# SyncE issues the second minus-maximum's rows ahead of two weight blocks, and the K parts lie in DRAM by dimension, batch and head

## What is computed

```
x = x + tanh(g_xattn[0]) * fp8_blockwise_product(layernorm(x), ctx)      # L0 "attention"
x = x + tanh(g_ffn[0])   * moe_8_experts_top2_plus_shared(layernorm(x))  # L0 feed-forward
x = x + tanh(g_xattn[1]) * causal_attention(layernorm(x), ctx, ctx)      # L1, 16 heads of 16
x = x + tanh(g_ffn[1])   * moe_8_experts_top2_hidden_1024(layernorm(x))  # L1 feed-forward
```

```
scores = einsum('bhqd,bhkd->bhqk', qh, kh) / 4
scores = where(causal, scores, -10000)
out    = einsum('bhqk,bhkd->bhqd', softmax(scores), vh)
```

## Time and profile before

| | us |
|---|---|
| median of 3 runs | 411.5 |
| lowest, highest | 411.11, 413.36 |
| the profiled execution | 412.41 |
| its span, first to last instruction | 410.6 |
| outside the span | 1.8 |
| DMA queue q1 (SyncE's), share of 16 engines | 40.2% |

### The profile page before, as it was taken

The page is one execution under the profiler, slowest core; times in us unless marked ns, Lnnn a source line. Parts: engine busy times, 40 slices in busy tenths (PEclk is TensorE's granted clock), DMA queues, the critical chain, the costliest instruction groups (busy, mean ns, idle before and its releaser), DMA issues.

```text
span 410.6 us, 8728 instructions
## 1 busy us (share of the span) xinstructions
PE 321.0 (78%) x2708; PEld 222.1 (54%) x2709; DVE 306.0 (75%) x745; ACT 268.2 (65%) x540; POOL 180.4 (44%) x245
## 2 busy tenths in 40 slices
PE   0075989989799986878777224698999999999991
PEld 0053337664377654556444113475777777777760
DVE  4998997783954663897998885586777777888760
ACT  1825766725676486989798665652677777777770
POOL 3051305391384067433747459410444554444432
PEclk9997999989989998999977756697999999999997
DMA  5950002851095069130416449455677777778522
GB/s 176 388 222 0 2 0 107 126 147 59 4 225 158 15 85 221 46 117 2 119 42 206 126 102 329 154 219 177 184 254 248 255 200 255 210 253 254 154 26 26
DMA packets 27298, 60.48 MB, mean 147 GB/s; under 512 B 4305, under 2 KB 17954, under 8 KB 24066
## 3 DMA queue, kind: packets, MB, share of 16 engines
q1 hardware_dynamic: 20658, 53.20, 40.2%
q0 software_dynamic: 4416, 6.13, 9.3%
q10 hardware_dynamic: 2192, 0.75, 0.7%
HBM read 29.00 MB, written 6.85 MB: 87 GB/s over the span
## 4 chain that ended last, share of the span: by engine, by line
PE 42%; DVE 28%; DMA 10%; issue 9%; ACT 8%; POOL 2%; ACTq 1%; SPq 0%; DVEq 0%; POOLq 0%
PE bank L1270 8%; PE bank L1637 6%; PE bank L1655 6%; DMA out_dram<-arena,SI 5%; DVE MX L2000 3%; PE bank L1640 3%; PE bank L1658 3%; DMA STG<-in_l_w_dram 2%; PE bank L1356 2%; PE bank L1231 2%; DMA arena<-NMS 2%; PE bank L1382 2%; DVE stats L1720 2%; PE bank L1378 1%; ACT arena L1131 1%
## 5 line engine op out<-in xcount | busy, mean ns | idle before, releaser
L1655 PE MATMUL bank<-arena 128*128 x184 | 63.4, 390 | 2.6 <-DVE X L2274 1.1
L1131 ACT ACTIVATE arena<-arena,B1D 128x128 f32<-128x128 f32 x184 | 57.4, 391 | 8.6 <-DVE arena L2287 8.1
L2287 DVE TENSOR_REDUCE arena<-bank 128x256 f32<-128x512 f32 x92 | 57.3, 680 | 3.1 <-PE bank L1640 3.1
L685 POOL TENSOR_TENSOR W<-STG,W 128x256 f16<-128x256 f32 x64 | 42.7, 700 | 33.4 <-ACT W L882 28.9
L782 POOL DMA_INDIRECT out_dram<-arena,SI x23 | 36.4, 1584 | 36.2 <-DMA out_dram<-arena,SI 16.9
L1658 PE MATMUL bank<-arena 128*128 x184 | 51.3, 279 | 0.0
L685 POOL TENSOR_TENSOR arena<-STG,arena 128x256 f16<-128x256 f32 x56 | 37.3, 700 | 30.2 <-ACT arena L882 28.8
L1637 PE MATMUL bank<-arena 128*128 128x256 f16 x256 | 46.4, 282 | 1.6 <-DVE arena L2250 1.6
L769 POOL DMA_INDIRECT arena<-token_rows,GI x23 | 22.8, 993 | 53.3 <-ACT WS L1125 45.1
L2292 DVE SCALAR_TENSOR_TENSOR arena<-arena 128x512 f16<-128x512 f32 x46 | 29.7, 688 | 21.8 <-ACT arena L1138 21.8
L1640 PE MATMUL bank<-arena 128*128 128x128 f16 x256 | 45.3, 225 | 0.0
(11 more groups left out here) (280 smaller groups left out, 722.3 us busy)
## 6 DMA issues: line engine op xcount, KB each, us to landing
STG<-in_l_w_dram SPq DMA_DIRECT2D x32, 512.0 KB, 4.0
arena<-W SPq DMA_DIRECT2D x16, 1024.0 KB
STG<-W SPq DMA_DIRECT2D x7, 1024.0 KB
arena<-in_l_w_dram SPq DMA_DIRECT2D x2, 1280.0 KB, 7.5
k_parts<-W SPq DMA_DIRECT2D x2, 768.0 KB, 4.4
arena<-k_parts SPq DMA_DIRECT2D x12, 128.0 KB, 5.2
X<-in_x_dram SPq DMA_DIRECT2D x2, 512.0 KB, 7.4
W<-in_ctx_dram SPq DMA_DIRECT2D x1, 1024.0 KB, 10.2
```

Of the source, the lines that this page charges most:

```text
L685: ins = nc.gpsimd.tensor_tensor(l, src, h, ALU.subtract)
L1131: ins = nc.scalar.activation(x, x, ACT.Gelu, bias=B1D[:, e, c:c + 1], scale=1.0 / (X_SCALE * W_SCALE))
L1655: nc.tensor.matmul(bank[6 + q][:, :], GDL[:, q, 0, c * P:(c + 1) * P], W2[:, e, c].rearrange("p s d -> p (s d)"), start=(c == 0), stop=Fal ...
L2287: v.tensor_reduce(half, o, AX.X, ALU.add).then_inc(s_dadd, 1)
```

## The change

Two edits. In SyncE's stream load_minus_max(1) now stands right behind stack 2, ahead of weight blocks 14 and 15. And the DRAM tensor k_parts gets the shape [part, dimension, batch, head, token]: what one row of a stack needs is 8 KB in one run, where it was 16 runs of 512 bytes. The store writes six DMAs, one for each half and part, with 512-byte runs (it was two DMAs with 2 KB runs), and the waits on it count to 96 instead of 32.

```diff
-        k_parts = nc.dram_tensor("k_parts", [3, D, N], BF16).ap()
+        k_parts = nc.dram_tensor("k_parts", [3, DH, B, HEADS, S], BF16).ap()
...
             for k in range(KC):
-                sp.dma_start(k_parts[:, k * P:(k + 1) * P, :].rearrange("s p n -> p s n"),
-                             KS[:, :, k]).then_inc(s_kparts_out, 16)
-            sp.wait_ge(s_kparts_out, 16 * KC)
+                for s in range(3):
+                    sp.dma_start(k_parts[s, :, :, k * HH:(k + 1) * HH].rearrange("d b h n -> h d b n"),
+                                 KS[:, s, k]).then_inc(s_kparts_out, 16)
+            sp.wait_ge(s_kparts_out, 48 * KC)
...
-                    src = k_parts[s, :, b * S:(b + 1) * S].rearrange("(h d) n -> d h n", d=DH)
+                    src = k_parts[s, :, b]
...
             sp.wait_ge(s_down, T)
             load_k_stack(2)
+            load_minus_max(1)
             for i in range(14, 16):
                 load_weights(i)
-            load_minus_max(1)
             load_k_stack(3)
...
-            pool.wait_ge(s_kparts_out, 16 * KC)
+            pool.wait_ge(s_kparts_out, 48 * KC)
...
-                    act.wait_ge(s_kparts_out, 16 * KC)
+                    act.wait_ge(s_kparts_out, 48 * KC)
```

## The result

| | before | after |
|---|---|---|
| median of the runs taken together, us | 412.89 (20 runs) | 414.96 (20 runs) |
| profiled execution, us | 412.41 | 416.61 |
| its span, us | 410.6 | 414.8 |
| outside the span, us | 1.8 | 1.8 |

The ratio after / before is 1.0065, 95% interval 1.0039 to 1.009. A median is of all executions of a kernel, a ratio of those alone in which the chip was not in its slower state, so the two need not agree exactly. The change costs 0.65%, some 2.7 us, where the forecast was +0.3 us, too little to be told from no change. On the prediction's scale (411.5) the ratio makes 414.2 us: above the forecast's own range of 409.5 to 413.7, and inside the range over all its cases. The two profiled executions differ by 4.2 us, more than the ratio says, so what follows takes from the two traces where time went and from the ratios how much it is.

A forecast was written before the change was run, and what follows sets the result against it. No engine bounds the kernel; the second minus-maximum's rows wait behind weight blocks in SyncE's queue. Order -2.35 us plus store +2.6 gives +0.25: 412.7 us profiled, 411.8 on the median's scale; own range 409.5 to 413.7, all cases 408.8 to 415.2.

The forecast's parts named there:

- the range over all its cases: Total time over the forecast and its rivals: 408.8 to 415.2 us, without the far tails of rivals 1 and 2.
- What bounds, and the slack: No engine bounds; the second minus-maximum's rows queue behind weight blocks, and the store may land by 78.4 us without stalling VectorE.
- Part 1, the order: SyncE's queue: rows ahead of blocks 14 and 15 land sooner; ScalarE's repeat limits the gain to 2.35 us (1.5 to 3.0).
- Part 2, the loads: K stack loads: 8 KB runs leave the rate as it is, since only 16 partitions take part; no time gained.
- for the sum it makes no difference: Stack loads: even if faster, rows land at 154.9 us and ScalarE still sets 157.72.
- Part 3, the store: K parts store: 8 engines, 30 ns a packet, seen at 80.9 us; VectorE loses 2.6 us.
- The sum: Whole kernel: -2.35 + 2.6 = +0.25 us, so 412.7 profiled, 411.8 on the scale of the runs' median.
- Rival 1: Store keeps all 16 engines, is seen at 75.2 us within the slack, only the gain remains: 409.2 us; chance 0.25.
- Rival 2: Store slower than 30 ns a packet through crowding; at 39 ns VectorE loses 6.0 us: 415.2 us; chance 0.2.
- Rival 3: The order's gain is taken back within the attention steps while the store's loss stays: 414.1 us; chance 0.1.
- What the prediction asked to look for: Rows issued first and landing in about 2 us, 3072 + 48 store packets, memset near 81, stack windows at 110 to 150 GB/s.

The follow-up runs named there:

- the order alone: Kernel before with only load_minus_max(1) moved ahead of weight blocks 14 and 15; k_parts keeps its old layout: 408.47 us, ratio 0.9917.
- the early value: Changed kernel with GpSimd computing batch 0's starting value before waiting for the store: 412.42 us, 0.9985; with block 9 also held back: 405.88 us, 0.9889.
- the wait on block 9: GpSimd holds block 9's low part until VectorE's minus maximum 0: on the changed kernel 411.14 us, 0.9956; on the kernel with only the order moved, 0.9894.
- the order with the wait: Kernel before with load_minus_max(1) moved and GpSimd's low part of block 9 held until VectorE's minus maximum 0: 409.05 us, ratio 0.9894.
- the 16-engine store: Kernel before, old order, k_parts padded so six DMAs store 512-byte runs with 128 rows outermost: 411.91 us, ratio 1.0012.
- the 2 KB store on 8 engines: Kernel before, old order, k_parts heads set apart by an unused row, so 8 heads are outermost with 2 KB runs: 415.98 us, ratio 1.0122.
- block 9 sooner: Kernel before with weight block 9 issued ahead of K stack 1 instead of behind it: 414.05 us, ratio 1.0054.

## Why the prediction was wrong

1. **What bounds, and the slack** (right). The wait for the rows was 4 us on TensorE and worth 2.3. The store's slack to 78.4 us is borne out from both sides: seen at 75.5, TensorE waits 1.71 us as before, seen at 79.5 it waits 3.20.
2. **Part 1, the order** (right). ScalarE's repeat sets what is left of the wait: forecast 2.35, measured 2.32 in the order-alone trace and 2.31 in the changed one. By the later rows the distance has grown: from stack 2 to the issue of the third rows the kernel before takes 29.79 us (177.06 - 147.27), the order alone 27.06 (172.96 - 145.90), 2.7 us less; over the traces of the seven kernels with the new order it is 27.06 to 28.25, of the five with the old one 29.30 to 31.63. The ratio says 3.4 (2.2 to 4.7), which takes in both 2.3 and 2.7.
3. **Part 2, the loads** (wrong in what it leaves out). The rate itself was nearly right: 16 partitions stay slow, 131 GB/s with 8 KB runs. Somewhat faster they are: the last of stack 0's six DMAs lands 5.5 us behind its issue where it took 6.8, and the second rows land 2.4 us (median) behind theirs in the changed kernel, 3.8 in the order alone. The Trainium skill (SBUF — State Buffer, Door 1: The DMA port swizzle) gives 104 GB/s for 16 partitions; the traces show 112, 131 and 145, so here it is the right size and no ceiling. But the sentence "for the sum it makes no difference" was checked only at the second rows. The load of stack 1 stands ahead of block 9 in the queue: from its issue to ScalarE's start on block 9 it was 123.67 - 112.16 = 11.51 us, and is now 125.97 - 116.53 = 9.44, and those 2.1 us closed a gap of 1.02. How much of it the loads do is not separated: the distance is 8.9 to 9.4 us in the three traces with the new layout and a late start, 10.5 and 10.9 in the two with the early value, and 10.6 to 11.9 in six of the seven with runs of 512 bytes in the loads (the seventh issues block 9 ahead of stack 1). The one with 10.57 has a gap of only 0.07.
4. **Part 3, the store** (right, and a little low). 8 engines, 29.8 ns a packet (30 taken), seen at 81.5 (80.9 forecast), VectorE late by 3.2 us (2.6). SyncE's six issues were put at 0.5 us each and took 7.71 in all, still inside the transfers. What the store is worth can be read from two kernels that have the wait on block 9 and differ only in the layout: 0.9956 - 0.9894 = 0.62%, 2.6 us (the intervals allow 0.4 to 4.7); against the order alone, 0.9917, it is 1.6 us. That the first equals the forecast's 2.6 is partly luck.
5. **The sum** (the step that failed). The step ended at TensorE's wait at 86.63 us and took for granted that a delay of 2.6 us travels to the end as 2.6 us. It lacks a term: what GpSimd's low parts meet on their way. That term measures 1.1% or 4.5 us (3.0 to 6.0) in the changed kernel and 4.0 us in the one with the early value, and 3.3 us in one pair of traces without the late store. The terms as they stand now, by ratios: -3.4 (order) + 2.6 (store) + 4.5 (block 9) = +3.7, against +2.7 measured, with 1.2, 2.1 and 1.5 us of uncertainty on them. The sum is no check of its own: the last two terms are steps from the order with the wait (-4.4) to the changed kernel, so with -4.4 in place of -3.4 it closes by construction.
6. **The rivals.** Rival 1 (16 engines) is refuted by the 48 completions, and the 16-engine store shows what it would have given. Rival 2 named a time near the measured one (415.2), but its mechanism is refuted: 39 ns a packet was 29.8. Rival 3 is refuted by the order alone. None of the three was what happened.
7. **What the prediction asked to look for** came true in the changed kernel (the second rows land in 2.0 to 2.8 us there, though in 3.5 to 4.2 in the order alone). This is how the missing term shows itself: every step as forecast and the end 2.4 us away means that a place was not looked at.

What remains open: the excess of the 2 KB store on 8 engines over its 1.5 us of waiting; how much of the second loss comes from block 9 landing sooner and how much from the step being shifted against the weight blocks (block 9 sooner, in the kernel before, makes 2.2 us); why a meeting with an unbroken run held VectorE's two operations for 1.04 us in the kernel with the early value and for 3.96 and 3.99 in others; and in how many executions of each kernel the meeting happens, since each has one trace. That holding block 9 back takes the loss away is shown; that the hold of VectorE is all of it is not.

## What to carry to other kernels

Follow a delay past the first wait that it lengthens, to the next place where two engines pass each other with a gap of about a us; a load that comes sooner can close such a gap, and so can a delay of the engine that waited for it. Before choosing a DRAM layout, count how many of the DMA engines its outermost dimension lets in, and compare the landing with the slack of whoever waits. Where a short reduction on VectorE is on the path, hold GpSimd's bulk work back with a wait on it: this cost nothing where the gap existed and gave 1% where it did not.

## What the runs showed of the hardware

- **VectorE beside GpSimd.** Two tensor_scalar operations on 128 x 16 numbers took 0.37 us with GpSimd idle (three traces). In the nine traces in which they met its run of tensor_tensor operations of 0.63 us each, they took 1.04 to 3.99 us, and in eight of the nine they ended 0.16 to 0.17 us behind the end of an unbroken stretch of the run: the 3.96 us lasted over six of GpSimd's operations, and 0.07 us without one was enough to end the hold in the 16-engine kernel. The ninth (the early value) got through in 1.04 us inside the run. The Trainium skill (SBUF — State Buffer, SBUF: two separate sides) calls the port pair that the two engines share an exclusive lock, held for a whole instruction, with the other side blocked. The traces agree that VectorE stops, and its operations of 0.58 to 0.60 us in the 16-engine kernel look like a turn taken at every boundary between GpSimd's instructions. But by the eight traces a turn at the next boundary is not to be counted on.
- **The size of packets and the number of engines.** 512-byte packets of a store from all 128 partitions took 28.2 ns on 16 engines and 29.8 on 8. What made the store slow was that half of the engines took part (seen at 75.5 on 16 engines, at 79.5 to 81.5 on 8).
- **The start of a store on 8 engines.** It moved 55 GB/s from 69 to 71 us and 167 from 71 to 76, and its six issues took 7.71 us of SyncE's queue, where those of the 16-engine store took 4.49.
- **The clock.** In the changed kernel TensorE's granted clock fell after idle times of 5.25 and 2.88 us, to a mean of 0.57 to 0.58 over 8 us and 0.62 over 4: 1.2 GHz for most of it. In the kernel before it fell to 0.66 over 4 us behind an idle time of 1.71 us. Between 112 and 120 us, behind an idle time of 2.1 us, it fell in the profiled executions of five of the twelve kernels and not in the others, so the clock of one profile there is no evidence for a change.
